# A three-layer hybrid block on one core: another order table and bank table, and the two-slot loop written out

## The reference

```python
x = x + attn_a(layernorm(x), Wq, Wk, Wv, Wo, bo)     # 16 heads of 64, causal, linear
x = x + ffn(layernorm(x), rhs)                        # int8 matmul with one scale a row and a column
x = x + attn_b(layernorm(x), q_w, k_w, v_w, ...)      # 16 heads of 32, rank-16 keys, a state that decays
x = x + ffn(layernorm(x), rhs)

# attn_a
q = relu(x @ Wq) + EPS; k = relu(x @ Wk) + EPS
context = cumsum(k v^T over time); k_cumsum = cumsum(k)
attn = (q context) / (q k_cumsum);  return attn @ Wo + bo
# attn_b
q, k = rope(x @ q_w.T), rope(x @ k_w.T); q_r = q Wq^T; k_r = k Wk^T; g = sigmoid(x @ g_w.T + g_b)
M = M * decay + (g k_r / sqrt(d)) v^T;  y = q_r M      # step by step along the sequence
h = x + y @ out_w.T + out_b;  return layernorm(h) * ln_g + ln_b
```

## Time and profile before

| | |
|---|---|
| median of 3 runs | 3141.79 us |
| the profiled execution | 3145.69 us |
| its span, first to last instruction | 3142.8 us |
| TensorE (PE) busy | 2945.4 us, 94% |
| TensorE weight loads (PEld) busy | 2207.3 us, 70% |
| VectorE (DVE) busy | 2220.4 us, 71% |
| GpSimd (POOL) busy | 1045.4 us, 33% |
| ScalarE (ACT) busy | 647.1 us, 21% |
| granted TensorE clock, mean | 0.991 |

### The profile page before, as it was taken

One profiled execution on the slowest core, in us unless ns is written; L12 is line 12 of the kernel. 1 busy time (PEld: TensorE's weight loads), 2 busy tenths in 40 slices (PEclk: granted clock), 3 DMA queues, 4 the chain that ended last, 5 costly groups with the idle time before them and its releaser, 6 DMA issues.

```text
span 3142.8 us, 126343 instructions
## 1 busy us (share of the span) xinstructions
PE 2945.4 (94%) x54866; PEld 2207.3 (70%) x54932; DVE 2220.4 (71%) x4958; ACT 647.1 (21%) x1165; POOL 1045.4 (33%) x1520
## 2 busy tenths in 40 slices
PE   3899999999999999999999999999999999999996
PEld 2677777777777777777777777777777767777674
DVE  7977777677676677676776677776766767767765
ACT  2222212212212212121212122122122122212211
POOL 2133423323333333333333233233233333333333
PEclk9999999999999999999999999999999999999998
DMA  5322222212122122122122121121121221121211
GB/s 172 79 49 48 46 45 48 46 43 48 44 44 46 44 47 43 42 48 48 42 48 48 42 48 45 44 48 44 43 46 44 47 43 43 47 48 42 48 41 31
DMA packets 384392, 153.91 MB, mean 49 GB/s; under 512 B 352800, under 2 KB 361632, under 8 KB 383904
## 3 DMA queue, kind: packets, MB, share of 16 engines
q1 hardware_dynamic: 383904, 146.05, 20.4%
HBM read 45.32 MB, written 16.78 MB: 20 GB/s over the span
## 4 chain that ended last, share of the span: by engine, by line
PE 92%; issue 4%; DVE 2%; DMA 1%; ACT 0%; POOL 0%; SPq 0%; POOLq 0%; DVEq 0%; ACTq 0%
PE bank L771 22%; PE bank L773 21%; PE bank L772 21%; PE bank L1049 7%; PE bank L912 3%; PE bank L729 2%; PE bank L850 2%; PE bank L836 2%; PE bank L868 2%; PE bank L883 2%; PE bank L980 2%; PE bank L1021 2%; PE bank L1004 1%; PE bank L1036 1%; DMA work<-in_L_attn_a_Wk 0%
## 5 line engine op out<-in xcount | busy, mean ns | idle before, releaser
L653 POOL TENSOR_TENSOR var_eps<-mean_var,column 128x1 f32<-128x1 f32 x320 | 107.2, 335 | 1362.7 <-DVE mean_var L1293 1362.7
L771 PE MATMUL bank<-xaT,wk_hi 128*128 128x128 f16 x2048 | 361.5, 221 | 0.0
L772 PE MATMUL bank<-xaT,wk_hi 128*128 128x128 f16 x2048 | 361.3, 221 | 0.0
L773 PE MATMUL bank<-xaT,wk_lo 128*128 128x128 f16 x2048 | 361.1, 221 | 0.0
L771 PE MATMUL bank<-xaT,wq_hi 128*128 128x128 f16 x2048 | 360.1, 220 | 0.0
L773 PE MATMUL bank<-xaT,wq_lo 128*128 128x128 f16 x2048 | 360.0, 220 | 0.0
L772 PE MATMUL bank<-xaT,wq_hi 128*128 128x128 f16 x2048 | 359.7, 220 | 0.0
L771 PE MATMUL bank<-xbT,wb 128*128 128x128 f16 x2048 | 346.6, 219 | 1.3 <-DMA xbT<-work 1.3
L772 PE MATMUL bank<-xbT,wb 128*128 128x128 f16 x2048 | 346.6, 219 | 0.0
L773 PE MATMUL bank<-xbT,wb 128*128 128x128 f16 x2048 | 346.5, 219 | 0.0
L771 PEld LDWEIGHTS bank<-xaT,wq_hi 128*128 128x128 f16 x2048 | 201.4, 98 | 62.6 <-issue 52.5
(11 more groups left out here) (204 smaller groups left out, 8086.3 us busy)
## 6 DMA issues: line engine op xcount, KB each, us to landing
xin<-in_L_attn_a_x SPq DMA_DIRECT2D x64, 256.0 KB, 2.6
out<-work SPq DMA_DIRECT2D x64, 256.0 KB, 2.0
table<-in_tables SPq DMA_DIRECT2D x64, 192.5 KB, 2.5
work<-in_L_attn_a_Wq SPq DMA_DIRECT2D x1, 2048.0 KB, 8.6
work<-in_L_attn_a_Wk SPq DMA_DIRECT2D x1, 2048.0 KB, 14.2
wb<-in_L_attn_a_Wv SPq DMA_DIRECT2D x1, 2048.0 KB, 18.8
work<-in_L_attn_a_Wo SPq DMA_DIRECT2D x1, 2048.0 KB, 8.1
work<-work SPq DMA_TRANSPOSE x128, 2.7
```

The costliest lines, as they stand in the source:

```text
L653: pool.tensor_tensor(var_eps[n][:, one], mean_var[n][:, c.par, 1:2], eps[:, :], ALU.add)\
L771: nc.tensor.matmul(o, a[0], b[0], start=first, stop=False)
L772: nc.tensor.matmul(o, a[0], b[1], start=False, stop=False)
L773: return nc.tensor.matmul(o, a[1], b[0], start=False, stop=last)
```

## The change

Three things change, all in the tables and in the function `run`.

1. `ORDER` is another list. The part-array steps of TensorE are spread: no run of them, uninterrupted by a full-array step, is longer than 96 matmuls of the trace. Lags change too; the largest is now 5 (`st_o`) where it was 4.
2. `BANK` gives the steps other banks; `LATE` and `BORROWED` (the preparation of the weights between the first slots) and `COUNTS` follow.
3. `run` has no loop: all 69 slots are written out with constant waits. `COUNTS` is not used any more.

The steps themselves are the same, with the same instructions.

```diff
-ORDER = [("x2l", 4), ("u0_e", 2), ("xTa_t", 1), ("xTb_l", 3), ("v0", 1), ("bias", 2), ("u1_e", 2), ("so0", 2),
-         ("so1", 2), ("out_e", 4), ("o0", 2), ("o1", 2), ("qk2", 1), ("no_st", 4), ("o0_e", 2), ("xTb_t", 3),
+ORDER = [("s", 2), ("so1", 2), ("nb_rs", 3), ("ld_t", 3), ("nb_ap", 3), ("xTb_h", 3), ("s_e", 2), ("xTb_l", 3),
+         ("x2l", 4), ("xTb_t", 3), ("out_e", 4), ("qk0", 1), ("so0", 2), ("o1", 2), ("o0", 2), ("o0_e", 2),
...
-BANK = {"v0": 6, "v1": 4, "qk0": 2, "qk1": 0, "qk2": 3, "qk3": 5, "kt0": 6, "s_a": 6, "s_b": 7, "o0a": 1, "o0b": 0,
+BANK = {"v0": 7, "v1": 7, "qk0": 6, "qk1": 7, "qk2": 6, "qk3": 0, "kt0": 3, "s_a": 7, "s_b": 1, "o0a": 2, "o0b": 3,
...
-            for s in range(FIRST_LOOP_SLOT):
-                walk(Slot(eng, s))
-            with nc.Fori(FIRST_LOOP_SLOT // 2, CHUNKS // 2, engines=[eng.engine], hint_back_edge=True) as it:
-                registers = {(per, const): eng.snap(it * per + const) for per, const in COUNTS[name_of]}
-                for n in range(2):
-                    walk(Slot(eng, n, it, registers))
-            for s in range(CHUNKS, CHUNKS + MAX_LAG):
+            for s in range(CHUNKS + MAX_LAG):
                 walk(Slot(eng, s))
```

More of the change, by code:

```diff
@@ L49 @@
 MAGIC = 1.5 * 2.0 ** 23
-ORDER = [("x2l", 4), ("u0_e", 2), ("xTa_t", 1), ("xTb_l", 3), ("v0", 1), ("bias", 2), ("u1_e", 2), ("so0", 2),
[4 rows of a table removed]
-         ("kb_a", 3), ("v0_e", 1), ("gb_e", 3), ("gb_s", 3), ("nf1_q", 4), ("wo_e", 2), ("nf0_st", 2), ("gb_k", 3),
[7 rows of a table removed]
-         ("nb_ap", 2), ("y_e", 3), ("ld_t", 2), ("u1", 1), ("u0", 1), ("s_e", 1), ("xTb_h", 2), ("out", 3)]
+ORDER = [("s", 2), ("so1", 2), ("nb_rs", 3), ("ld_t", 3), ("nb_ap", 3), ("xTb_h", 3), ("s_e", 2), ("xTb_l", 3),
+         ("x2l", 4), ("xTb_t", 3), ("out_e", 4), ("qk0", 1), ("so0", 2), ("o1", 2), ("o0", 2), ("o0_e", 2),
+         ("qk1", 1), ("o1_e", 2), ("qk3", 1), ("kb", 3), ("aT0_h", 2), ("aT0_l", 2), ("qb", 3), ("aT1_h", 2),
+         ("qk0_e", 1), ("bias", 2), ("no_st", 4), ("no_rs", 4), ("st_o", 5), ("aT0_t", 2), ("no_ap", 4),
+         ("aT1_l", 2), ("no_f", 4), ("nf1_st", 4), ("qk2", 1), ("kb_e", 3), ("aT1_t", 2), ("qk1_e", 1),
+         ("nf1_rs", 4), ("gb", 3), ("nf1_ap", 4), ("qb_e", 3), ("kb_a", 3), ("gb_e", 3), ("kb_h", 3), ("gb_s", 3),
[8 rows of a table added]
+         ("nb_st", 2), ("xTa_t", 0)]
 LAG = dict(ORDER)
@@ L70 @@
 MAX_LAG = max(LAG.values())
-BANK = {"v0": 6, "v1": 4, "qk0": 2, "qk1": 0, "qk2": 3, "qk3": 5, "kt0": 6, "s_a": 6, "s_b": 7, "o0a": 1, "o0b": 0,
-        "u0a": 0, "u0b": 4, "kt1": 7, "o1a": 4, "o1b": 5, "u1a": 1, "u1b": 5, "wo": 2, "mm0": 4, "qb": 7, "kb": 5,
-        "vb": 7, "gb": 0, "qr": 2, "kr": 3, "sb0": 0, "sb1": 7, "sb2": 5, "sb3": 1, "y0": 2, "y1": 3, "ub0": 6,
-        "ub1": 4, "out": 2, "mm1": 1}
+BANK = {"v0": 7, "v1": 7, "qk0": 6, "qk1": 7, "qk2": 6, "qk3": 0, "kt0": 3, "s_a": 7, "s_b": 1, "o0a": 2, "o0b": 3,
+        "u0a": 2, "u0b": 6, "kt1": 6, "o1a": 4, "o1b": 5, "u1a": 3, "u1b": 4, "wo": 1, "mm0": 5, "qb": 3, "kb": 2,
+        "vb": 2, "gb": 4, "qr": 4, "kr": 0, "sb0": 3, "sb1": 5, "sb2": 2, "sb3": 4, "y0": 0, "y1": 1, "ub0": 5,
+        "ub1": 1, "out": 0, "mm1": 4}
 BANKS = 8
@@ L95 @@
 LATE = {
[L96 to L141, removed]
+    (0, "qk1_e"): ("load o",),
@@ new lines @@
+    (0, "nf1_ap"): ("max o",),
+    (0, "qb_e"): ("turn decay",),
+    (0, "qb_a"): ("all o",),
+    (0, "sb"): ("scale o",),
+    (0, "xTa_l"): ("hi o", "keep decay"),
+    (1, "no_st"): ("lo o",),
+    (1, "no_ap"): ("load g",),
+    (1, "nf1_q"): ("load rk",),
+    (1, "ld_x"): ("load rhs",),
+    (1, "xTa_l"): ("max rhs",),
+    (1, "u1"): ("all rhs",),
+    (1, "u0_e"): ("columns of rhs",),
+    (1, "u1_e"): ("rows of rhs",),
+    (1, "mm0_a"): ("load bk",),
+    (2, "nb_rs"): ("scale rhs",),
@@ new lines @@
+    (2, "xTb_t"): ("round rhs",),
+    (2, "qb"): ("load rq",),
+    (2, "bias"): ("load bq",),
+    (2, "aT1_l"): ("max bk",),
+    (2, "nf1_rs"): ("all bk",),
+    (2, "wo0"): ("scale bk", "max bq"),
+    (2, "qk3_e"): ("max g",),
+    (2, "wo_e"): ("all g", "max rk"),
+    (2, "kr"): ("all bq",),
+    (2, "ld_x"): ("scale bq",),
+    (2, "kT"): ("scale g",),
+    (2, "kt0_e"): ("hi bk",),
+    (2, "ub_m"): ("all rk",),
+    (2, "kT_e"): ("hi bq",),
+    (2, "ys1"): ("scale rk",),
+    (2, "sb_e0"): ("max rq",),
@@ L142 @@
+    (2, "na_ap"): ("lo bk",),
+    (2, "u1_e"): ("all rq",),
+    (2, "out"): ("hi g",),
+    (2, "nb_st"): ("lo bq", "hi rk"),
+    (3, "nb_rs"): ("load bv",),
+    (3, "xTb_t"): ("scale rq",),
+    (3, "qk3"): ("hi rq", "lo g"),
+    (3, "bias"): ("lo rk",),
+    (3, "no_rs"): ("max bv", "all bv"),
+    (3, "qk1_e"): ("scale bv",),
+    (3, "nf1_rs"): ("lo rq",),
+    (3, "nf1_ap"): ("hi bv",),
+    (3, "kb_h"): ("lo bv",),
+    (3, "qb_a"): ("load wout",),
 }
 TAKEN = ("q", "k", "v", "o", "rhs", "bk", "bq", "g", "rk", "rq", "bv")
[L146 to L155, removed]
+BORROWED = {"decay": (0, "qb_e", 0),
+            "o": (0, "qb_a", 4),
+            "rhs": (1, "u1", 5),
+            "rhs rows": (1, "u1_e", 6),
+            "bk": (2, "nf1_rs", 3),
+            "g": (2, "wo_e", 0),
+            "bq": (2, "kr", 1),
+            "rk": (2, "ub_m", 1),
+            "rq": (2, "u1_e", 0),
+            "bv": (3, "no_rs", 5)}
@@ L170 @@
 COUNTS = {
-    "SP": [(2, -3), (2, -2), (2, -1), (2, 0), (2, 1), (8, -4), (8, 0), (10, -14), (10, -9), (10, -5), (10, -4),
-           (10, 0)],
-    "POOL": [(2, -3), (2, -2), (2, -1), (2, 0), (2, 1), (2, 2), (6, -7), (6, -4), (6, -1), (8, -5), (8, -4), (8, -1),
[6 rows of a table removed]
[L180 to L183, removed]
[4 rows of a table removed]
+    "SP": [(2, -4), (2, -3), (2, -2), (2, -1), (2, 0), (2, 1), (2, 2), (8, -9), (8, -8), (8, -5), (8, -4), (8, -1),
+           (12, -17), (12, -11)],
+    "POOL": [(2, -3), (2, -2), (2, -1), (2, 0), (2, 1), (2, 2), (8, -7), (8, -6), (8, -4), (8, -3), (8, -2), (8, 0),
[6 rows of a table added]
+    "ACT": [(2, -3), (2, -2), (2, -1), (2, 0), (2, 1), (2, 2), (8, -10), (8, -8), (8, -7), (8, -6), (8, -4), (8, -3),
[3 rows of a table added]
+    "DVE": [(2, -4), (2, -3), (2, -2), (2, -1), (2, 0), (2, 1), (2, 2), (4, -3), (4, -2), (4, -1), (4, 0), (8, -7),
[4 rows of a table added]
 }
```

## The result

The changed kernel takes 3029.77 us (median of three runs, 3029.63 to 3031.03) against 3141.79 before: a ratio of 0.964, with an interval of 0.962 to 0.966. The forecast was 3047, with a range from 3034 to 3075. The sign and the mechanism came out as forecast; the time lies 17 us under the forecast and 4 us under the low end of the range: the sizes of three terms of the sum were off.

What follows compares the result with a forecast made beforehand. TensorE, stopped by instruction fetch, bounds the kernel. A slot becomes 45.27 + 0.2 + 0.31 + 0.1 = 45.88 us instead of 47.72; 54 slots gain 99, less 2: 3045, stated as 3047, range 3034 to 3075.

Steps and rivals of the forecast that it cites:

- Part 2: Part-array runs of at most 96: written-out slots' idle falls from 0.64 to 0.2 us; the sum also keeps 0.1 hidden stops.
- base of 45.27 us: TensorE's mean busy time a slot over six written-out slots of the kernel before, the start of the sum.
- Part 3: Steps between full-array and part-array matmuls on TensorE: four runs become six, +0.31 us a slot, +20 us over 64 slots.
- What bounds the kernel: TensorE, busy 94% of the span; in the loop hardly anything but "issue" ends its idle time, no engine is late.
- What the stops are: Long part-array runs drain TensorE's instruction store; packets of some 268 instructions come at best 4.0 us apart.
- Part 1: Removing the loop (27 jumps back, register work) saves 1.81 us a slot, alone 98 us over 54 slots.
- Part 4: New order may surface waits, nearest `kr_e` for `ub` on VectorE, 0.6 us left; covered by 1.1 us, cost 0.
- A: Rival: stops stay as in the written-out slots, idle 0.64, hidden 0.1 more; 46.3 us a slot, 3071 us; chance 0.14.
- B: Rival: the clock still falls, seven times or twice as often, +12 to +24 us, 3059 to 3071; chance 0.12.
- C: Rival: idle is not fetching but something loop removal leaves alone; only +0.31 a slot remains, 3162 us; chance 0.02.
- D: Rival: TensorE waits for `khat_ready` every slot because VectorE is late; 3205 us if 4 us late; chance 0.04.
- idle 0.14, no hidden stops: Low end of the forecast's own range, 3036 us, with the idle of the quickest written-out slot in view.

Runs made afterwards that it cites:

- b_pad: Kernel before with 128 one-semaphore increments on TensorE ahead of its first slot, moving later packet boundaries: 3156.35 us, ratio 1.003.
- the length tests: Changed kernel with products of u0, u1 carried out twice: run of 128, 3110.12 us; with mm0 also ahead of yb: 160, 3068.82; 192, 3139.86.
- b_flat: Kernel before with only its loop written out, old order, banks and weight preparation kept: 3076.45 us, ratio 0.982.
- a_mm0: Changed kernel with mm0 ahead of yb, so yb, u0 and u1 make one run of 128, five runs a slot: 3025.02 us, ratio 0.961.
- a_split: Changed kernel with qk1 between o1 and o0, so one run of 96 becomes 64 and 32, seven runs a slot: 3046.69 us, ratio 0.968.
- a_run192: Changed kernel with qk0 moved behind o0, so two runs of 96 become one run of 192: 3086.6 us, ratio 0.984.
- a_len192: Changed kernel with mm0 ahead of yb and u0 and u1 both carried out twice, one run of 192: 3139.86 us.

## Why the prediction was right or wrong, point by point

What failed is the size of three terms of the sum: the 0.3 us of stops left by Part 2, where the runs showed none; the base of 45.27 us, where a stop-free slot takes 45.11; and the 0.31 of Part 3, where the order costs 0.48.

- **What bounds the kernel**: right. No other engine became late in the full slots; idle time before part-array lines was the thing to remove.
- **What the stops are**: right in kind, shown by `b_pad`, the places of the stops and the length tests. The packet's size was taken as 268 instructions; the places say 256. The packets' closest distance was taken as 4.0 us from a single view; it is 3.0 us in that same trace and 3.3 in `b_flat`, so the supply is somewhat better than the 67 instructions a us of Part 2. That no stop remained fits this.
- **Part 1, no loop**: wrong in size. 98 us forecast for it alone, 64 measured. The step that failed is the comparison of the loop with six written-out slots "since these differ in nothing else". They differed in where the boundaries fell; the mean written-out slot of that order is 46.34 us, not 45.91. It did little harm to the sum, which takes the new slot from 45.27 and not from this difference.
- **Part 2, shorter runs**: right in direction, too small. I let 0.2 us of idle and 0.1 of hidden stops remain. Nothing remained: 0.30 us a slot, 19 us, the largest part of the miss.
- **Base of the sum**: 45.27, a busy time with hidden stops in it, instead of the 45.11 us of a stop-free slot in the same trace: 0.16 us a slot, 10 us.
- **Part 3, changes of mode**: right for what it counted (0.31 against 0.34, and `a_mm0` and `a_split` confirm the price with 0.23 and 0.27 a run), but the new order costs 0.48. The 0.15 at `sb`, the transposes behind it and `u0`, `u1` was missing: 0.17 us a slot, 11 us the other way.
- **Part 4, dependencies**: right. `kr_e` for `ub` was never waited for in the full slots. `a_run192` shows what a lost cover costs, 0.6 us a slot, at another place than the one I watched.
- **Rivals**: A, the stops staying as they are, did not come. `b_flat` at 3076 lies near A's 3071 by chance: A holds 20 us of changes of mode that `b_flat` does not have, and without them it says 3051. B, falls of the clock, did not come: the changed kernel runs at 1.00 from 112 to 2952 us. The falls go with the stops: `a_len192` brought them back, at 496.10 us at the stop shown above. (The forecast's seven falls in the loop are six: the seventh in that trace, at 3082 us, lies behind the loop.) C, the idle time not being fetching, and D, a wait for `khat_ready`, did not occur.
- **The range**: its low end of 3034 stands just under the 3036 of "idle 0.14, no hidden stops" on the base of 45.27. A low end from the stop-free slot (45.11 + 0.31, no stops) is 45.42, some 3018 us. The bound was built from the quickest slot looked at, not from the quickest in the trace.

## What to carry to other kernels

When a cost depends on where something falls (a packet's boundary, a phase against the slot), a few neighbouring slots are one throw: list all of them, take the minimum as the floor and the mean over a whole period as the expectation, and build the low end of the range on the floor. Count the part-array matmuls, each with its weight load, over a few microseconds rather than per run, and keep them under the supply, here 256 instructions every 3.0 to 4 us; a full-array step between two runs must last long enough for the next packet. Past that point each further split costs 0.23 to 0.27 us, so the best order has the fewest runs that still don't stop: 96 was shorter than needed, and merging two runs to 128 gained 5 us more.
